# First layer of a graph network: messages summed in windows of PSUM and folded into SBUF, attentions as a column of the messages, target rows read by VectorE from two PSUM banks

## The reference

```python
h = relu(layernorm(x))
for _ in range(2):
    edge_feat = concatenate([h[src], h[dst]], axis=-1)
    messages  = relu(edge_feat @ msg_W1 + msg_b1) @ msg_W2 + msg_b2
    att       = sigmoid(relu(edge_feat @ att_W1 + att_b1) @ att_W2 + att_b2)
    aggregated = segment_sum(messages * att, dst)          # one row per node
    combined  = concatenate([h, aggregated], axis=-1)
    new_h     = relu(combined @ upd_W1 + upd_b1) @ upd_W2 + upd_b2
    h = new_h + h + global_repr
x = x + h
# layers 1, 2 and 3 follow: a sum over neighbours, and two attentions over edges
```

## Time and profile before

| what | value |
|---|---|
| timed runs, median of 3 | 6965.2 us (6962.06 to 6969.63) |
| the profiled execution: span from first to last instruction | 8811.7 us |
| the profiled execution: its own time outside the span | not shown |
| busy in the span: PE, DVE, ACT, POOL | 5601.3, 4821.7, 1551.7, 4885.4 us |
| mean granted clock of TensorE | 0.693 of 2.4 GHz |
| indirect DMAs on POOL: layer 0 / all of the five large groups | 1664 / 4550 |

### The profile page before, as it was taken

The page is one execution under the profiler, slowest core; times in us unless marked ns, Lnnn a source line. Parts: engine busy times, 40 slices in busy tenths (PEclk is TensorE's granted clock), DMA queues, the critical chain, the costliest instruction groups (busy, mean ns, idle before and its releaser), DMA issues. The chain is left out here.

```text
span 8811.7 us, 137163 instructions
## 1 busy us (share of the span) xinstructions
PE 5601.3 (64%) x29121; PEld 4731.6 (54%) x29122; DVE 4821.7 (55%) x17321; ACT 1551.7 (18%) x4108; POOL 4885.4 (55%) x4627
## 2 busy tenths in 40 slices
PE   6555555677776767767769999566666665333334
PEld 5555554466666656666655666366666654322223
DVE  5555554355555545555548888445454444444445
ACT  1111111122222222222222222100000002000001
POOL 2555555466666356666626777244444442666564
PEclk6555555788878878788779999755555566555556
DMA  5444444333333233333323444233333333333332
GB/s 162 94 94 93 94 95 105 109 100 100 97 100 98 61 103 98 99 97 96 97 53 59 62 62 60 85 87 87 87 82 85 85 86 56 75 74 75 73 73 51
DMA packets 919114, 759.39 MB, mean 86 GB/s; under 512 B 585479, under 2 KB 750483, under 8 KB 916979
## 3 DMA queue, kind: packets, MB, share of 16 engines
q0 software_dynamic: 233264, 421.09, 20.3%
q1 hardware_dynamic: 677068, 327.25, 15.5%
q10 hardware_dynamic: 8704, 10.11, 0.3%
HBM read 676.11 MB, written 80.55 MB: 86 GB/s over the span
## 5 line engine op out<-in xcount | busy, mean ns | idle before, releaser
L1300 POOL DMA_INDIRECT there<-table_wide,idx x1664 | 1748.0, 1050 | 1163.5 <-issue 666.1
L1413 PE MATMUL ps<-here,hot_t 128*128 x3328 | 1178.3, 487 | 784.4 <-ACT near L1373 666.8
L2404 POOL DMA_INDIRECT there<-table_wide,idx x832 | 791.6, 951 | 964.9 <-DVE msg L2480 474.2
L1331 DVE TENSOR_SCALAR hot_s<-iota,loc,att 128x128 f32<-128x128 f32 x1664 | 546.1, 374 | 1224.2 <-ACT att L1383 597.0
L1413 PEld LDWEIGHTS ps<-here,hot_t 128*128 128x128 f32 x3328 | 704.7, 235 | 910.9 <-issue 804.4
L709 POOL DMA_INDIRECT rec<-out_recd,posd x806 | 802.7, 996 | 598.6 <-ACT out_recd L689 322.6
L3023 POOL DMA_INDIRECT there<-table_narrow,idx x832 | 791.0, 951 | 613.1 <-issue 243.7
L3180 PE MATMUL ps<-here,hot_t 128*128 x1664 | 407.4, 422 | 852.1 <-DVE prod L3104 486.5
L1373 ACT ACTIVATE near<-ps 128x512 f32<-128x512 f32 x832 | 497.0, 597 | 2105.3 <-PE ps L1413 1028.4
L1421 PE MATMUL ps<-relu,hot_s 128*128 128x128 f32 x3328 | 838.3, 343 | 6.5 <-DVE hot_s L1331 4.7
L3180 PEld LDWEIGHTS ps<-here,hot_t 128*128 128x128 f32 x1664 | 354.4, 306 | 905.8 <-issue 905.7
(11 more groups left out here) (511 smaller groups left out, 10174.1 us busy)
## 6 DMA issues: line engine op xcount, KB each, us to landing
locrows<-loc_row SPq DMA_DIRECT2D x416, 256.0 KB
krowd<-key_row SPq DMA_DIRECT2D x201, 256.0 KB
there<-table_wide,idx POOLq DMA_INDIRECT x2496
src_rows1a<-slot_src_row SPq DMA_DIRECT2D x52, 512.0 KB
lrowd<-lo_row SPq DMA_DIRECT2D x201, 128.0 KB
attr_raw<-in_edge_attr SPq DMA_DIRECT2D x201, 128.0 KB
there<-table_narrow,idx POOLq DMA_INDIRECT x832
rec<-out_recd,posd POOLq DMA_INDIRECT x806
```

The lines of the kernel that those rows point to most:

```text
L1300: nc.gpsimd.indirect_dma_start(there[:, j, q, :], None, table, bass.IndirectOffsetOnAxis(idx[:, j, q:q + 1], 0)).then_inc(gathered[j][q], 16)
L1413: last = nc.tensor.matmul(ps[:, WORK, (q % 2) * 2 * F:(q % 2 + 1) * 2 * F], hot_t[:, j % 2, q * P:(q + 1) * P], here[:, :, :].rearrange("p ...
L2404: nc.gpsimd.indirect_dma_start(there[:, j, q, :], None, table, bass.IndirectOffsetOnAxis(idx[:, j, q:q + 1], 0)).then_inc(gathered[j][q], 16)
```

## The change

Four things change in `attention_messages`, and `collect` and `sorted_index` follow.

- **Windows.** The sums no longer have a place of their own in PSUM for each block. Each chunk of a group gets a slot of `F + H` = 136 columns, three slots to a bank, in one of two windows of three banks. The slot is the block's number less that of the group's first chunk; `sorted_index` works out its column for every chunk (`g["window"]`, five more DVE instructions). A group that spans n blocks so uses n slots of its window.
- **Folds.** When a group's matmuls are done, DVE adds the window's 8 slots to `acc` in SBUF (`fold`, two additions of 774 and 258 elements), at the place of the group's first block, a register that DVE loads from `g["block"]`. ACT then writes zeros to the window (`clear`).
- **Attentions as a column.** `relu` has 129 columns, of which the last is 1.0; one matmul of 129 columns takes the place of one with 128 and one with 1.
- **No copies.** PE makes the target rows in two banks in turn (6 and 7), DVE's sum reads them there; `near` and `copied` go. PE now adds group j-1 where it added group j-2, and makes the target rows two pairs ahead.

`collect` transposes `acc` directly. In `sort_edges` the number of chunks of a block is at least 1, so that the blocks of a group follow one another without a hole.

```diff
+            groups = g["block"][:, :].rearrange("o (n u) -> o n u", u=U)
+            nc.vector.tensor_tensor(rank.rearrange("o (n u) -> o n u", u=U), groups, groups[:, :, 0:1].to_broadcast([1, NV // U, U]),
+                                    ALU.subtract).then_inc(ranked, 1)
+            dve.wait_ge(ranked, 1)
...
+SLOT = F + H
+SLOTS_OF_BANK = 512 // SLOT
+WINDOW = 3
+FIRST = SLOTS_OF_BANK * SLOT
+REST = U * SLOT - 2 * FIRST
...
-        near = c.sb("near" + tag, [P, 2, U, 2 * F])
-        relu = c.sb("relu" + tag, [P, 2, U, F])
+        relu = c.sb("relu" + tag, [P, 2, U, F + 1])
...
+            nc.vector.memset(relu[:, :, :, F:F + 1], 1.0).then_inc(blank, 1)
+            nc.vector.memset(acc[:, :, :], 0.0).then_inc(blank, 1)
...
+            def fold(i, j, first):
+                start = nc.values_load_multi_w_load_instructions(g["block"][0:1, ds(i * CH + j * U, 1)], engines=[mybir.EngineType.DVE],
+                                                                 min_val=0, max_val=NB - 1, skip_runtime_bounds_check_because=
+                                                                 "sort_edges counts the node blocks begun: 1 to NB, less one")[1][0]
+                b = j % 2
+                flat = acc[:, :, :].rearrange("p t f -> p (t f)")
+                dve.wait_ge(added, i * CH + (j * U + 3 * U))
+                if first:
+                    dve.wait_ge(blank, 2)
+                else:
+                    dve.wait_ge(folded, i * (2 * RING) + 2 * j)
+                many = 2 * SLOTS_OF_BANK
+                whole = flat[:, ds(start * (F + 1), many * (F + 1))].rearrange("p (n m f) -> p n m f", n=2, f=F + 1)
+                window = ps[:, WINDOW * b:WINDOW * b + 2, 0:FIRST].rearrange("p n (m f) -> p n m f", f=SLOT)
+                nc.vector.tensor_tensor(whole, whole, window[:, :, :, 0:F + 1], ALU.add).then_inc(folded, 1)
+                rest = flat[:, ds(start * (F + 1) + many * (F + 1), (U - many) * (F + 1))].rearrange("p (m f) -> p m f", f=F + 1)
+                window = ps[:, WINDOW * b + 2, 0:REST].rearrange("p (m f) -> p m f", f=SLOT)
+                nc.vector.tensor_tensor(rest, rest, window[:, :, 0:F + 1], ALU.add).then_inc(folded, 1)
+
+            def combine(i, j, before, older, after, first):
-                    dve.wait_ge(copied, i * (RING * PR) + (j * PR + m + 1))
+                    dve.wait_ge(spread, i * (RING * PR) + (2 * PR + j * PR + m + 1))
                     pair = there[:, j, 2 * m:2 * m + 2, :]
-                    nc.vector.tensor_tensor(pair, pair, near[:, j % 2, 2 * m:2 * m + 2, :], ALU.add).then_inc(summed, 1)
+                    nc.vector.tensor_tensor(pair, pair, ps[:, TARGETS + m % 2, :].rearrange("p (q f) -> p q f", q=2), ALU.add).then_inc(summed, 1)
                     if m:
                         dot_att(i, j, m - 1)
+                    if m == 1 and older is not None:
+                        fold(*older, first)
...
+            for j in range(RING - 2, RING):
+                fold(LOOPS - 1, j, False)
...
-            def copy_pair(i, j, m, first):
-                act.wait_ge(spread, i * (RING * PR) + (2 * PR + j * PR + m + 1))
-                if not first:
-                    act.wait_ge(summed, i * (RING * PR) + (j * PR + m + 1 - 2 * PR))
-                nc.scalar.activation(near[:, j % 2, 2 * m:2 * m + 2, :], ps[:, WORK, :].rearrange("p (q f) -> p q f", q=2), ACT.Copy).then_inc(copied, 1)
...
+            def clear(i, j):
+                b = j % 2
+                act.wait_ge(folded, i * (2 * RING) + (2 * j + 2))
+                nc.scalar.activation(ps[:, WINDOW * b:WINDOW * b + 2, 0:FIRST], k["zeros4"][:, None, 0:FIRST].to_broadcast([P, 2, FIRST]), ACT.Copy)
+                nc.scalar.activation(ps[:, WINDOW * b + 2, 0:REST], k["zeros4"][:, 0:REST], ACT.Copy).then_inc(cleared, 1)
+
+            def group(i, j, older):
                 act.wait_ge(added, i * CH + (j * U + U))
                 for m in range(PR):
-                    if ahead is not None:
-                        copy_pair(*ahead, m, first)
                     act.wait_ge(summed, i * (RING * PR) + (j * PR + m + 1))
-                    nc.scalar.activation(relu[:, j % 2, 2 * m:2 * m + 2, :], there[:, j, 2 * m:2 * m + 2, 0:F], ACT.Relu).then_inc(cut, 1)
+                    nc.scalar.activation(relu[:, j % 2, 2 * m:2 * m + 2, 0:F], there[:, j, 2 * m:2 * m + 2, 0:F], ACT.Relu).then_inc(cut, 1)
+                    if m == 2 and older is not None:
+                        clear(*older)
...
             def target_pair(i, j, m, blocks, first):
                 if not first:
-                    pe.wait_ge(copied, i * (RING * PR) + (j * PR + m))
+                    pe.wait_ge(summed, i * (RING * PR) + (j * PR + m - 1))
                 for q in (2 * m, 2 * m + 1):
-                    last = nc.tensor.matmul(ps[:, WORK, (q % 2) * 2 * F:(q % 2 + 1) * 2 * F], hot_t[:, j % 2, q * P:(q + 1) * P],
+                    last = nc.tensor.matmul(ps[:, TARGETS + m % 2, (q % 2) * 2 * F:(q % 2 + 1) * 2 * F], hot_t[:, j % 2, q * P:(q + 1) * P],
                                             here[:, :, :].rearrange("p t f -> p (t f)")[:, ds(blocks[q] * (2 * F), 2 * F)],
                                             start=True, stop=True, skip_group_check=True)
                 last.then_inc(spread, 1)
 
-            def add_pair(i, j, m, blocks):
+            def add_pair(i, j, m, columns):
+                if m == 0:
+                    pe.wait_ge(cleared, i * RING + (j + 1))
                 for q in (2 * m, 2 * m + 1):
                     pe.wait_ge(weighted, i * CH + (j * U + q + 1))
-                    nc.tensor.matmul(wide(ps)[:, ds(blocks[q] * F, F)], hot_s[:, j % 2, q, :], relu[:, j % 2, q, :],
-                                     start=False, stop=True, skip_group_check=True)
-                    nc.tensor.matmul(wide(ps)[:, ds(blocks[q] + NP, 1)], hot_s[:, j % 2, q, :], k["ones"][:, 0:1],
+                    nc.tensor.matmul(wide(ps)[:, ds(columns[q] + WINDOW * 512 * (j % 2), F + 1)], hot_s[:, j % 2, q, :], relu[:, j % 2, q, :],
                                      start=False, stop=True, skip_group_check=True).then_inc(added, 1)
 
-            def half_step(now, before):
-
+            def columns_of(i, j):
+                return load_blocks(nc, g["window"], i * CH + j * U, U, 2 * 512 + REST - SLOT)
+
+            def begin_targets(i, j):
+                blocks = load_blocks(nc, g["block"], i * CH + j * U, U, NB - 1)
+                pe.wait_ge(hots, i * RING + (j + 3))
+                return blocks
+
+            def half_step(now, before, after):
+
+                if before is not None:
+                    columns = columns_of(*before)
                 if now is not None:
-                    blocks = load_blocks(nc, g["block"], now[0] * CH + now[1] * U, U, NB - 1)
-                    pe.wait_ge(hots, now[0] * RING + (now[1] + 3))
+                    blocks = begin_targets(*now)
                 for m in range(PR):
-                    if now is not None:
-                        target_pair(*now, m, blocks, before is None and m == 0 and now[1] == 0)
-                    if before is not None and m == 0:
-                        blocks_before = load_blocks(nc, g["block"], before[0] * CH + before[1] * U, U, NB - 1)
                     if before is not None:
-                        add_pair(*before, m, blocks_before)
-
-            half_step((0, 0), None)
-            half_step((0, 1), None)
-            for j in range(2, RING):
-                half_step((0, j), (0, j - 2))
-            with pe.Fori(1, LOOPS) as i:
+                        add_pair(*before, m, columns)
+                    if m + 2 < PR:
+                        if now is not None:
+                            target_pair(*now, m + 2, blocks, False)
+                    elif after is not None:
+                        if m + 2 == PR:
+                            blocks_after = begin_targets(*after)
+                        target_pair(*after, m + 2 - PR, blocks_after, False)
...
-        rows = c.sb("acc_rows" + tag, [P, NP])
...
+            nc.vector.tensor_copy(sums[:, :].rearrange("p (t o) -> p t o", o=1), acc[:, 0:NB, F:F + 1])
-                last = nc.tensor.transpose(wide(ps)[:, t * P:(t + 1) * P], rows[:, t * P:(t + 1) * P], k["ident"][:, :])
+                last = nc.tensor.transpose(wide(ps)[:, t * P:(t + 1) * P], acc[:, t, 0:F], k["ident"][:, :])
```

More of the change, by code:

```diff
@@ L1367, in _ @@
             act.sem_inc(gated, 2)
[L1369 to L1375 removed]
+            act.sem_inc(cleared, 2)
@@ L1383, in group, with step @@
                 nc.scalar.activation(att[:, j % 2, :], dot[:, j % 2, :], ACT.Sigmoid, bias=w["att_b2"][:, 0:1]).then_inc(gated, 1)
-            def after(i, j):
-                return (i, j + 1) if j + 1 < RING else (i + 1, 0)
-            for m in range(PR):
-                copy_pair(0, 0, m, True)
+            def step(i, j, n):
+                return (i + (j + n) // RING, (j + n) % RING)
```

(12 more changed lines are left out.)

63 lines of the change are left out of this document (34 added, 29 removed).

## The result

| | before | after |
|---|---|---|
| median of 4 runs, us | 6963.6 (6955.5 to 6969.6) | 6875.1 (6863.6 to 6887.9) |
| ratio of after to before | | 0.9876, 95% [0.9864, 0.9888] |
| profiled execution: its time, us | | 6878.1 |
| its span, us | 8811.7 | 6876.0 |
| mean granted clock | | 0.764 |

The change makes the kernel 1.2% faster. The direction is the forecast one, the size is 44% of it; 6875 lies in the range of 6600 to 6985, and at the very edge of the likeliest case's own range of 6640 to 6880.

What follows compares the result with a forecast made beforehand. The prediction took POOL's gathers to bound layer 0's two sweeps in timed runs. Its terms, -160 - 40 - 2 + 2 = -200 us, took 6965 to 6765 us, with a range of 6600 to 6985 us.

Steps and rivals of the forecast that it cites:

- the likeliest case: The main forecast for the whole kernel: 6765 us, own range 6640 to 6880, chance 61%.
- What bounds the kernel: Layer 0's two sweeps: POOL's gathers bound them in timed runs, which lose nearly all of POOL's profiled waits.
- Part 1: Layer 0's sum L1342 reads PSUM and no longer holds up gathers: -160 us, bounds -90 and -200.
- The group before, 10.8 us: Layer 0 sweeps before the change: eight gathers at 1.052 us plus 0.30 us pause each, 10.8 us a group.
- Part 2: Layer 0's target rows: no ACT copies and two banks cut POOL's waits for slots, -40 us, between 0 and 540.
- Part 3: Message matmuls: the ones column drops 1664 matmuls, PE's half-clock group 13.5 to 10.0 us; part of the 40 us.
- Part 4: Folds on DVE: its group grows to 8.8 us, range 8.5 to 9.1, under POOL's pace: 0 us.
- Part 5: Clearing windows on ACT: under 3 x 0.60 us a group, where ACT lost 4 x 0.60: 0 us.
- Parts 6 and 7: Sweep ends, with blanking of `acc`: -2 us; five window-number instructions before the node kinds: +2 us, bounds 0 and +5.
- A, the copy loop is real: Layer 0 rival: timed runs have the late hand-overs too, 6285 us at most, 6500 for a good half; chance 12%.
- B, DVE becomes the bound: Layer 0 rival: gathers need 8.8 us a group, DVE 9.4 after the change, +125 us, 7090; chance 19%.
- C, the disturber is another: Layer 0 rival: L1323 or the hot rows lengthen gathers, which stay at 1050 ns; nothing measurable, 6965 us; chance 8%.

Runs made afterwards that it cites:

- experiment 1: The kernel before, unchanged, run again with a second profile: 6959.2 us, span 6957.5 us.
- experiment 2: The kernel before, with only ACT's copies removed and the sum reading its target rows from the one PSUM bank: 6875.8 us against 6956.6, ratio 0.9889.
- experiment 3: The changed kernel with ACT's copies put back, so the sum reads an SBUF tile: 6970.1 us against the kernel before's 6956.6, ratio 1.0020.
- experiment 7: The changed kernel with the attentions' column in a matmul of its own again: 6874.9 us, ratio 0.9885 to the kernel before.
- experiment 5: The changed kernel plus one 774-element DVE add from PSUM a group: 6866.3 us against the kernel before's 6955.0, ratio 0.9875.
- experiment 6: The changed kernel plus two 774-element DVE adds from PSUM a group: 6915.0 us, ratio 0.9948 to the kernel before.
- experiment 9: The changed kernel plus one DVE copy of 1024 columns from SBUF to SBUF a group: ratio 0.9917 to the kernel before.
- experiment 10: The changed kernel plus one DVE add of 1024 columns a group, both operands in SBUF: ratio 0.9998 to the kernel before.
- experiment 4: The changed kernel plus one DVE fill of 2800 columns a group: 7272.9 us, ratio 1.0459 to the kernel before.

## Why the prediction was right in kind and wrong in size

*What bounds the kernel*: right. POOL's gathers bound both sweeps in ordinary executions; the waits of the first profile (274 us a sweep) are not in them (experiment 1). The budget of POOL's work led there: 4833 us of indirect DMAs then, 4777 in the ordinary profile.

*Part 1, the operand, -160 us (bounds -90 to -200)*: the mechanism is right, from both sides (experiments 2 and 3). The size is where the prediction failed: it measured -79 us, below my lower bound. Two steps of it were wrong. First, "layer 0's gathers take 1050 ns against 951" was carried as 99 ns over to the timed runs. It is a property of that execution: in an ordinary one they take 1002, against 945 with DVE idle. The 140 us that I gave to L1342 fit the first profile (144 counted); in the ordinary one it is 72. I had argued that this profile's waits were not real, and still took its durations as real. A held gather's length depends on when it is issued within the sum, so it is itself a matter of timing. Second, "an L1342 is met more often, up to x 1.25" had the wrong sign: 419 met it in the stretched profile, 281 in the ordinary one. With POOL as the bound, DVE waits for the gather's data, and where it does, the sum tends to begin while the next gather is already running, which does no harm: of 567 sums that DVE had waited for, 108 had a gather issued inside them, of the other 265 there were 201. In the stretched profile DVE had waited for 8 of 832. In experiment 3, where DVE idles 108 us ahead of its sums instead of 493, 446 gathers met one. What decides the meetings is how the two engines lie in time, not the rate.

*The group before, 10.8 us*: 10.46, by the same mistake; after, 10.1, is 10.07.

*Part 2, no copies, two banks, -40 us (0 to -540)*: 0, the other term that was too large. POOL's idle time is the same, and one bank does as well (experiment 2). The lower bound was right; having just argued that POOL bounds the sweep, I should have taken it.

*Part 3, ones column*: 0, not a part of 40 (experiment 7). That PE was over POOL's pace at half clock did not matter: its 741.54 busy us of 890 left it free in the ordinary profile.

*Part 4, folds 0 us*: right. 956 and 416 ns against 0.96 and 0.42; no stall ahead of them shows (0.0 us idle), so the load of the register must lie beside the products. DVE's group is 8.73 us, forecast 8.5 to 9.1. The reserve is real (experiment 5) and ends where it should (experiment 6), but what lies over it first fills the ring and shows at a sweep's end.

*Part 5, clearing*: right, 837 and 382 ns on an ACT that is busy 268 of 890 us.

*Parts 6 and 7*: 0 together in the forecast; the spans leave 81.5 - 79.4 = 2 us for all that isn't gathers, too little to tell. The five window instructions take 0.58 to 1.01 us each, as worked out, and the fill of `acc` 3.50 us where I said 4.3.

*What was to show it*: gathers at 955 (said 960 to 985), group 10.07, DVE busy 87% of the stretch (said 80). The span of 8150 to 8650 for the profile of after did not come: its execution was an ordinary one.

*Rivals.* A, the copy loop is real: no, ordinary executions don't have its waits. B, DVE becomes the bound: needs 1.3 us more of work a group. C, the disturber is another: no; hot rows hold no gather (208 issued inside them, 950 ns), and of the product only 18 us came.

The corrected sum is 208 groups x (10.46 - 10.07) = 81 us, or 1664 x 47 ns = 78.

What stays open: why the first profile's execution was stretched (that its signals were late, as I read the earlier trace rows, no run shows), why the fill and the copy hold gathers, and why they can stop one that is running where an add can't. The Trainium skill ("GPSIMD Engine Reference", section 8, Key points) has two kinds of DVE instruction that contend with GpSimd: two SBUF inputs, and 2-port performance modes. By this rule the sum is of the first kind, and the trace agrees (281 gathers at 1203 ns). The copy could only be of the second. The trace fits that: undisturbed it takes 686 ns for 1024 columns, the add 1217 ns for as many. That it ran in such a mode no run here shows by itself. The fill has no input in SBUF and takes 2392 ns for 2800 columns; which kind it would be is not shown either. My reading of that rule's second half in the prediction, that it would keep the hot rows as a disturber, did not come true.

## What to carry to other kernels

When a profile's span is far from the timed runs, take over none of its numbers that depend on how engines meet in time; not the waits, and not the durations of instructions that others can hold. Compare a stage's duration with the instruction's own undisturbed rows (DVE idle or reading PSUM), and look at several executions before sizing the gain. And when one queue bounds a stage, ask only what shortens that queue's items: moving one operand to PSUM was the whole gain, and it could be had in two stages for a few lines.

## What the runs showed of the hardware

- A gather's issue on GpSimd takes 0.945 to 0.95 us, if DVE is idle or runs an add with one operand in PSUM. Issued inside an add of two SBUF operands or a copy between SBUF tiles, it ends 0.81 to 0.83 us after that instruction's end (experiments 9 and 10); inside a fill, 0.89 us after, which makes 2.87 us in the mean for a fill of 2.39.
- A gather that is already running is not touched by an add that starts later (177 cases in experiment 10, 0.96 us at most). A copy that starts 0.2 to 0.52 us into it stops it, and so does a fill in its first 0.4 us (experiments 9 and 4); a copy that starts 0.52 to some 0.75 us into it is itself made longer, up to 0.94 us instead of 0.69.
- An fp32 fill on DVE, which reads nothing, cost more here than any add: 2.4 us of it a group cost 406 / 208 = 1.95 us a group (experiment 4).
- The sum of 128x512 is no slower with one operand in PSUM: 681 ns (changed kernel) against 689 (before, second profile).
- POOL's pause of 0.305 us behind each indirect DMA is the same in layer 0, in the sort and in layers 2 and 3 of the changed kernel's profile (median 0.305 us in each).
